# Exponentials of step two moved three chunks up in the bodies with four adjacency units (graph layer with top-p attention, one core)

## What is computed

```
R = (S + I) / row sums
for n in range(2):
    q = Xa @ W1.T @ W2.T;  k = Xa @ W3.T
    probs = softmax(q @ k.T)                 # rows of 3327
    A = probs, kept to the largest that make up 0.9 of a row, scaled to sum 1
    Xf = R @ Xf;  Xa = A @ Xa
    Z += Xf @ U1[n].T + Xa @ U2[n].T
h = layernorm(X + Z) * ln_g + ln_b
out = layernorm(x + h)
```

## Time and profile before

| what | value |
|---|---|
| median of 3 runs | 1439.35 us (1435.52 to 1441.99) |
| the profiled execution | 1437.9 us, its span 1436.1 us |
| DVE busy | 1288.7 us (90%) |
| PE busy | 1229.3 us (86%) |
| ACT busy | 921.2 us (64%) |
| POOL busy | 354.1 us (25%) |
| mean granted TensorE clock | 0.934 of full speed |

### The profile page before, as it was taken

How to read it: one execution, slowest core, us unless ns; L and a number is a source line. 1 busy time by engine, 2 the same in 40 slices (tenths; PEclk the granted TensorE clock), 3 DMA queues, 4 the chain that set the end, 5 groups by cost and what they waited for, 6 DMA issues and landing times.

```text
span 1436.1 us, 29717 instructions
## 1 busy us (share of the span) xinstructions
PE 1229.3 (86%) x9162; PEld 1037.9 (72%) x9162; DVE 1288.7 (90%) x7002; ACT 921.2 (64%) x1974; POOL 354.1 (25%) x584
## 2 busy tenths in 40 slices
PE   7899999999997989997999796919894965929896
PEld 3677777777785977887888786818784765828796
DVE  5799889988984898999989999899999998999995
ACT  4887888788757555755575655636664635636764
POOL 0221232123200341313141220202332312312242
PEclk9999999999998999998999898959997997969998
DMA  5000000000021440412132131211412031211311
GB/s 204 1 2 2 2 2 2 2 2 2 2 97 48 151 184 11 182 49 96 54 139 96 48 134 60 97 48 49 144 49 96 16 129 49 86 59 50 144 49 48
DMA packets 16599, 96.49 MB, mean 67 GB/s; under 512 B 1251, under 2 KB 8930, under 8 KB 9730
## 3 DMA queue, kind: packets, MB, share of 16 engines
q1 hardware_dynamic: 16384, 94.14, 18.6%
HBM read 92.43 MB, written 1.70 MB: 66 GB/s over the span
## 4 chain that ended last, share of the span: by engine, by line
PE 44%; DVE 37%; ACT 11%; issue 5%; POOL 1%; DVEq 1%; DMA 0%; SPq 0%; ACTq 0%; POOLq 0%
PE bank L616 25%; DVE cand L833 13%; PE bank L595 11%; DVE junkC L890 8%; PE bank L550 5%; ACT E L691 4%; DVE E L1232 2%; ACT blkT L716 2%; ACT cand L686 2%; DVE sub L1054 2%; DVE E L1234 1%; PE bank L631 1%; DVE junkS L890 1%; DVE slots L953 1%; ACT S L691 1%
## 5 line engine op out<-in xcount | busy, mean ns | idle before, releaser
L716 ACT ACTIVATE blkT<-bank 128x512 f32<-128x512 f32 (+1 forms) x728 | 406.7, 565 | 283.0 <-PE bank L595 279.0
L833 DVE MAX8 cand<-E 128x8 f32<-128x32 f32 (+1 forms) x2992 | 404.4, 192 | 37.2 <-ACT E L667 22.7
L616 PEld LDWEIGHTS bank<-X,blkT 128*128 128x128 f32 x2704 | 330.3, 192 | 107.8 <-ACT blkT L716 76.3
L616 PE MATMUL bank<-X,blkT 128*128 128x129 f32 (+1 forms) x2704 | 377.5, 282 | 13.9 <-ACT blkT L716 12.7
L595 PE MATMUL bank<-ident,S 128*128 128x128 f32 x1560 | 243.3, 276 | 16.0 <-POOL S L447 14.2
L595 PE MATMUL bank<-ident,E 128*128 128x128 f32 x1144 | 182.1, 284 | 81.9 <-DVE E L1234 81.9
L890 DVE SCALAR_TENSOR_TENSOR junkC<-cand,st 128x128 f32<-128x128 f32 (+2 forms) x390 | 241.1, 626 | 2.4
L616 PE MATMUL bank<-YF,blkT 128*128 128x128 f32 x1352 | 193.0, 287 | 43.1 <-ACT blkT L716 43.1
L616 PEld LDWEIGHTS bank<-YF,blkT 128*128 128x128 f32 x1352 | 172.5, 199 | 74.7 <-ACT blkT L716 63.6
L550 PE MATMUL bank<-kT,Q 64*128 64x512 f32 (+1 forms) x728 | 197.2, 614 | 7.9 <-ACT E L667 7.6
L595 PEld LDWEIGHTS bank<-ident,E 128*128 128x128 f32 x1144 | 142.8, 148 | 84.0 <-DVE E L1234 82.8
(11 more groups left out here) (222 smaller groups left out, 1336.2 us busy)
## 6 DMA issues: line engine op xcount, KB each, us to landing
S<-in_adj_dram SPq DMA_DIRECT2D x50, 1663.5 KB, 7.0
S<-in_adj_dram SPq DMA_DIRECT2D x2, 1455.6 KB, 8.1
X<-in_x_dram SPq DMA_DIRECT2D x6, 256.0 KB, 4.1
out_dram<-H SPq DMA_DIRECT2D x1, 1408.0 KB
S<-in_adj_dram SPq DMA_DIRECT2D x2, 194.9 KB, 9.9
u_in<-in_L_gnn_U_dram SPq DMA_DIRECT2D x4, 64.0 KB, 9.5
out_dram<-H SPq DMA_DIRECT2D x1, 128.0 KB
w_in<-in_L_gnn_W_dram SPq DMA_DIRECT2D x2, 32.0 KB, 2.0
```

The source lines that it names most:

```text
L616: m = pe.matmul(bank[int(u.acc)][:, 0:width], blkT[:, slot, b * P:(b + 1) * P], rhs[:, j, 0:width], start=(j == 0), stop=(j == NT - 1))
L716: act.activation(blkT[:, slot, 0:w], BLK[early][slot][:, 0:w], ACT.Copy).then_inc(blk_done, 1)
L833: v.max(cand[:, par, xx, 8 * r:8 * r + 8], E[where_e[self.s, self.p]][:, xx, r * w:min((r + 1) * w, N)]).then_inc(s_max, 1)
```

## The change

A constant is added, and the pieces of the exponentials in bodies with four R units stand at i = 33 to 38 in place of 36 to 41. Nothing else changes: bodies with three R units, step one, the number of instructions, the buffers and the semaphores stay.

```diff
     STEP_R = [4, 3] * 6 + [0]
+
+    EXPS_AHEAD = 3
...
             for k in range(6):
-                b.exps.setdefault(5 * NCH + 1 + (k if STEP_R[p] > 3 else 0), []).append((1, p + 2, k))
+                b.exps.setdefault(5 * NCH + 1 + (k - EXPS_AHEAD if STEP_R[p] > 3 else 0), []).append((1, p + 2, k))
```

## The result

The changed kernel takes 1450.01 us (median, 1446.54 to 1451.98) where the kernel before took 1438.83 us beside it: a ratio of 1.0079, 95% interval 1.0062 to 1.0096. It is slower, by 11 us, where about 1 us was forecast, and lies outside the range. The profiled execution has a span of 1449.0 us against 1436.1 us.

The account below looks back on a forecast made before the run. VectorE (90% busy) and TensorE (86%) bound it together, handing over to each other. -0.4 (two waits) + 0 (bodies 0, 2) + 0 (4, 8) - 0.1 (6) + 1.7 (10) = +1.2 on 1439.35: 1440.6 us, range 1433 to 1447.

Parts of the forecast that it names:

- Removed: two waits of VectorE: Searches of pairs 2 and 4: waits of 5.8 us in total go, 0.2 us kept each, -0.4 us.
- Rival A: The removed waits of VectorE are gains that stay: 1432.6 us, chance 0.11.
- Moved: copies behind pieces, in bodies 0 and 2: ScalarE's copies come behind pieces, TensorE waits about 2.5 us for `newT`: 0 us, bounds -0.4 and +1.5.
- a sign of being wrong: Profile after: TensorE's clock falls in bodies 0 and 2 and their length grows by more than 1 us.
- The case that the prediction built beside the Trainium skill's rule: Bodies 0 and 2 pay 1.5 us each for the slow clock, the sum 3.0 us more.
- In bodies 4 and 8 ... So nothing: TensorE ends these bodies at most 3.8 us later, covered by its wait for `settle`: 0 us.
- body 6 at -0.1: Maxima ready about as the wait moves to them: -0.1 us, between 0 and -0.9.
- Body 10, +1.7 us: ScalarE waits for pair 12's maxima before piece 0, body 11 starts later: +1.7 us, bounds 0 and 3.8.
- Rival B: Waits halve TensorE's clock in bodies 0, 2, 6 and 10, plus body 10's 1.7 us: 1447.1 us, chance 0.13.
- The sum: All parts of the change together: +1.2 us, 1440.6 us for the median.
- the prediction's own limit of 0.5%: About 7.2 us, what a measurement can tell from no change; slower was given 0.07.

Follow-up runs that it names:

- the kernel with bodies 0 and 2 alone: Exponentials three chunks up in bodies 0 and 2 only, against the kernel before: 1.0023, 1440.29 us.
- the single experiments: Exponentials three chunks up in one group of bodies, against the kernel before: 0 and 2 1.0023; 4, 6 and 8 1.0064; 10 1.0014.
- the kernel where only that one was lost: The kernel before, no exponential moved, load of S behind each even body's last unit held back by one chunk: 0.9999, 1437.45 us.

## Why the prediction was wrong

- *"Removed: two waits of VectorE", kept 0.2 us each.* Right in what happens. The waits went and came back as 3.70 and 3.71 us before L835. Against the start of bodies 1 and 3 the settles of pairs 2 and 4 come 0.6 us earlier, where 0.2 was forecast, and since these bodies start later, nothing of it is left. Rival A is out for the changed kernel, by the kernel with bodies 0 and 2 alone. Its condition, earlier logits, was met in one kernel and didn't help by time (0.9990 against 0.9991). But with `out_mul` later the kernel with the earlier exponentials is 0.25% better than the one without, so that they are worth nothing anywhere is not shown.
- *"Moved: copies behind pieces, in bodies 0 and 2", 0 us with a bound of +1.5.* The step failed by its choice in the range. The wait for `newT` was forecast at 2.5 us and is 2.31, with some luck: it was worked out from an end of TensorE's own work at 732.6 us that no row gives (by the earlier trace rows TensorE was done 0.95 us before 732.85). What was priced at nothing is what the wait does to the clock. The bound, +1.5 each, was worked out from a wait of about the same length, and 1.8 and 1.6 us came. The prediction had named this as a sign of being wrong: the clock falls in bodies 0 and 2 and they grow by more than 1 us. By time the two bodies cost 0.23%, 3.3 us, and all of it went with the wait. The case that the prediction built beside the Trainium skill's rule that activity releases the slow clock level (TensorE: Matmul & The Clock Gate, part 1) gave the better number here, +3.0 us for both, and the trace agrees with the rule: the slow stretch stands right behind the idle time.
- *"In bodies 4 and 8 ... So nothing", and body 6 at -0.1.* This is the step that made the forecast wrong, 0.64% by time. It named TensorE's late end as the cost and `settle` as its cover, and the cover held: TensorE still waits 30.64 us before body 6. But the last transposes release a load of S, and the forecast did not follow that DMA. The load ran into VectorE's branch, and VectorE, which TensorE waits for here, stood idle for 2.45 us behind it, 2.83 us at pair 8 and 2.46 us at pair 10. The earlier trace rows had the same thing in small, 0.93 us; I read it as an oddity of the small step. The bound was off too: 3.8 us at the most for the later end of a body, where body 4 takes 4.5 us more.
- *Body 10, +1.7 us.* Right: 2 us by time, with 3.55 us of wait for the maxima where 3.9 were worked out.
- *Rival B* named the clock in bodies 0 and 2, which was right, and in body 10, where the trace doesn't show it: the granted clock is 1.00 from 1357 to 1360 us. It came nearest with 1447.1 us, but that is luck in part: of its 7.7 us the 3.0 for the clock in bodies 6 and 10 did not come, and body 6 takes 73.6 us where it took 73.7. The mechanism that cost most was in no case. By the prediction's own limit of 0.5% the result is slower, to which it gave a chance of 0.07.
- *The sum.* Forecast +1.2 us. By the single experiments: 3.3 (bodies 0 and 2, forecast 0) + 9.2 (4, 6 and 8, forecast -0.1) + 2.0 (body 10, forecast 1.7) = 14.5, and 11.2 as measured for all together.

## What to carry over

When a step on one engine is moved, follow what the late instructions release as far as the DMAs, and lay each DMA's new time beside the places where other engines branch. "Hidden behind another engine's wait" covers the engine, not the transfers that it triggers. And where a change gathers an engine's small waits into one, price the slower clock behind it whenever that engine has the pace.

## What the runs showed of the hardware

- VectorE's program comes by DMA in packets (queue q14 here), and a packet can wait behind data. With a 1.7 MB load of S in the queues (99.4% of the packet time) no instruction packet came through, and VectorE stood idle for 2.12 to 2.86 us after a branch, marked "issue" in the profile (twice put down to ScalarE's sums). With the queues free, the profile lists no idle time in the same place. That the packets are VectorE's is read from their times: the idle time ahead of this line ended 1.94 to 2.00 us behind the start of a packet each time.
- Free queues are no guarantee at other branches: at 1189.30 us in the kernel before VectorE had stood idle for 2.34 us with no load of S in the queues, and the packet that ended it began 1.87 us before.
- Such a wait can be taken back: of 2 us lost at one branch, 1.5 came back by the next settle in the kernel where only that one was lost.
- A wait of TensorE of 2.31 us was followed by a granted clock of 0.76 over the next 7 us in body 2, one of 0.95 us in the same place by the full clock. The length of one wait alone doesn't tell it: the same wait of 2.02 us for S in body 10 was followed by a granted clock of 1.00 over the next 4 us in the kernel before and of 0.57 in three of the experiments' kernels.
